# A three-block transformer kernel: weights ahead of tokens on the load queue, per-group waits for the first slots, and the first row maxima closed one phase earlier

## The reference

```python
x = x + 0.5 * L0_ffn(_layernorm(x))     # mixture of experts
x = x + L0_attn(_layernorm(x))          # causal softmax attention, 16 heads of width 16
x = x + 0.5 * L0_ffn(_layernorm(x))     # the same mixture of experts, same weights
x = x + 0.5 * L1_ffn(_layernorm(x))     # gated feed-forward with fp4-quantised activations and weights
x = x + L1_attn(_layernorm(x))          # causal linear attention
x = x + 0.5 * L1_ffn(_layernorm(x))
```

## Time and profile before

| | us |
|---|---|
| median of 3 executions | 2094.27 |
| lowest and highest | 2093.43, 2095.04 |
| the profiled execution | 2094.46 |
| its span in the trace | 2092.8 |
| PE busy, share of the span | 1996.7, 95% |
| DVE busy | 1478.9, 71% |
| ACT busy | 987.8, 47% |
| POOL busy | 927.5, 44% |
| end of the first-layer phase on PE (from the span's start) | 422.7 |
| first instruction of PE in the attention phase | 434.7 |
| end of the attention phase on PE | 910.3 |
| last slot's up_proj in the second layer begins | 1250.9 |

### The profile page before, as it was taken

How to read it: one execution, slowest core, us unless ns; L and a number is a source line. 1 busy time by engine, 2 the same in 40 slices (tenths; PEclk the granted TensorE clock), 3 DMA queues, 4 the chain that set the end, 5 groups by cost and what they waited for, 6 DMA issues and landing times.

```text
span 2092.8 us, 41681 instructions
## 1 busy us (share of the span) xinstructions
PE 1996.7 (95%) x13717; PEld 1400.7 (67%) x13717; DVE 1478.9 (71%) x4068; ACT 987.8 (47%) x2304; POOL 927.5 (44%) x1139
## 2 busy tenths in 40 slices
PE   6999999979999999987999998999999999899998
PEld 5999996534444444356899995776766666567776
DVE  6432555778888888643467648998877777698884
ACT  2333334346666666742334433333347777543432
POOL 5423655331111121213432566555557676556553
PEclk9999999989999999997999999999999999999999
DMA  6556655634443455013465662000000000000000
GB/s 199 199 196 211 241 203 136 167 62 54 62 59 46 51 62 62 2 45 136 135 209 194 222 203 68 1 0 0 1 1 2 2 2 2 2 11 20 10 21 21
DMA packets 101711, 173.59 MB, mean 83 GB/s; under 512 B 14704, under 2 KB 66320, under 8 KB 101520
## 3 DMA queue, kind: packets, MB, share of 16 engines
q1 hardware_dynamic: 95376, 154.40, 28.1%
q0 software_dynamic: 6144, 16.79, 2.3%
HBM read 136.01 MB, written 34.87 MB: 82 GB/s over the span
## 4 chain that ended last, share of the span: by engine, by line
PE 38%; DVE 13%; issue 3%; POOL 1%; ACT 1%; DVEq 0%; DMA 0%; SPq 0%; ACTq 0%; POOLq 0%
PE s_Y L805 5%; PE s_HH L793 5%; PE s_Y L1924 5%; PE s_R L1894 4%; PE s_HH L1894 4%; PE s_HH L2248 2%; PE s_R L2235 2%; PE s_Y L2327 1%; PE s_Y L2319 1%; DVE ff_hscale L1607 1%; DVE s_HH L1787 1%; PE s_R L2283 1%; DVE fw_down L1610 1%; PE s_R L2269 1%; PE s_R L1916 1%
## 5 line engine op out<-in xcount | busy, mean ns | idle before, releaser
L1023 DVE TENSOR_REDUCE part_max<-a_psS 128x1 f32<-128x512 f32 (+3 forms) x570 | 340.2, 655 | 74.2 <-PE a_psS L1016 66.1
L1558 ACT ACTIVATE a_PT<-a_psE 128x512 f32<-128x512 f32 (+1 forms) x608 | 308.9, 583 | 153.7 <-PE a_psE L1448 136.6
L1418 POOL TENSOR_SCALAR_AFFINE_SELECT a_PT<-a_PT 128x512 f32<-128x512 f32 x128 | 81.2, 634 | 376.4 <-ACT a_PT L1558 376.4
L1837 POOL TENSOR_TENSOR fw_down<-fw_down,ff_hm 128x704 f32<-128x704 f32 x64 | 97.4, 1522 | 226.2 <-DVE fw_down L1619 222.3
L1859 ACT ACTIVATE ff_hm<-fw_down 128x704 bf16<-128x704 f32 x64 | 50.6, 790 | 286.2 <-DVE fw_down L1610 286.2
L1924 PE MATMUL s_Y<-w_down,fw_up 128*128 128x256 f32 x768 | 178.0, 382 | 3.9 <-DVE X L1804 3.0
L1894 PE MATMUL s_R<-w_gate,ff_xqT 128*128 128x512 f32 (+1 forms) x512 | 165.7, 467 | 10.0 <-ACT ff_sil L1869 10.0
L1894 PE MATMUL s_HH<-w_up,ff_xqT 128*128 128x512 f32 (+1 forms) x512 | 162.5, 460 | 2.1 <-DVE fw_down L1610 2.1
L1924 PEld LDWEIGHTS s_Y<-w_down,fw_up 128*128 128x128 f32 x768 | 145.1, 191 | 21.4 <-issue 3.2
L1448 PE MATMUL a_psE<-sq,sk 98*128 98x512 bf16 (+3 forms) x528 | 153.3, 328 | 2.3 <-ACT a_PT L1558 1.4
L1464 PE MATMUL a_psO<-a_PT,a_va 128*32 128x512 f32 (+3 forms) x1536 | 150.4, 494 | 2.5 <-POOL a_PT L1418 1.8
(11 more groups left out here) (498 smaller groups left out, 4369.1 us busy)
## 6 DMA issues: line engine op xcount, KB each, us to landing
e_w<-w_in SPq DMA_DIRECT2D x35, 1024.0 KB, 5.0
sq<-w_in SPq DMA_DIRECT2D x18, 1024.0 KB, 5.1
sk<-w_in SPq DMA_DIRECT2D x17, 1024.0 KB, 5.1
e_xs<-sorted_x SPq DMA_DIRECT2D x70, 128.0 KB, 3.9
e_xr<-sorted_x SPq DMA_DIRECT2D x70, 128.0 KB, 4.3
sorted_y<-e_yo SPq DMA_DIRECT2D x70, 128.0 KB
sq<-qk_parts SPq DMA_DIRECT2D x66, 128.0 KB, 5.9
sk<-qk_parts SPq DMA_DIRECT2D x66, 128.0 KB, 6.4
```

The costliest lines, as they stand in the source:

```text
L1023: return dve.tensor_reduce(st.part_max[:, c, h0:h0 + heads, qt], scores[:, 0:heads * n].rearrange("p (h k) -> p h k", h=heads), AX.X, ALU.max)
L1418: pool.affine_select(out=hidden, in_=hidden, compare_op=ALU.is_ge, fill=0.0, base=0, pattern=[[0, HG], [1, P]], channel_multiplier=-1).the ...
L1558: act.activation(PT[kt % 2][:, h0:h0 + heads, q0:q0 + n], psE[e % RING][:, 0:heads * n].rearrange("p (h q) -> p h q", h=heads), ACT.Exp, s ...
L1837: c.link(pool.tensor_tensor(hv[i], hv[i], hm[i][:], ALU.subtract))
```

## The change

There are five edits.

1. The wait of the first slots is split. `scattered_first`, one semaphore for the first 12 (or 16) tiles, becomes one per group of four tiles. `load` of slot t waits for group (t + 3) // 4, each group once.
2. In `experts` the stage `load_weights` now stands ahead of `load` at the same depth, for all slots of both layers, and it takes over the wait for `ordered`.
3. SP stores hi as soon as `high` is there and mid as soon as `rest` is there. Only low still waits for `cut`; before, all three did.
4. Block 0's maxima are closed, turned, copied and stored in the first-layer phase, and the 9 lead pieces of block 1 are done there too. The score stages become 48 with start 4.6 and pace 0.1, instead of 38 with 4.8 and 0.11. The attention phase starts with its exponentials.
5. The semaphores are cleared, with the barrier behind that, only after the attention phase and at the end; the clearing and its barrier behind the setup and behind the first-layer phase are gone. The blocks' own barriers stay.

The core of the diff:

```diff
@@ -438,7 +440,7 @@
             if t % G == 0:
                 pool.wait_ge(placed, PLACED * (t // G + 1))
             pool.indirect_dma_start(st.sorted_x[:, :], bass.IndirectOffsetOnAxis(ap=st.slot[:, t:t + 1], axis=0),
-                                    XN[:, t, :], None).then_inc(scattered_first if t < FIRST_TILES else scattered, 16)
+                                    XN[:, t, :], None).then_inc(scattered_group[t // G] if t < FIRST_TILES else scattered, 16)
 
         return [(J, root, G), (J + 11, scatter)]
...
-    parts.scattered_first, parts.scattered = (scattered_first, 16 * FIRST_TILES), (scattered, 16 * (TILES - FIRST_TILES))
+    parts.scattered_group = [(s, 16 * G) for s in scattered_group]
+    parts.scattered = (scattered, 16 * (TILES - FIRST_TILES))
+    parts.filled_by = lambda slot: (slot + EXPERTS - 1) // G
...
@@ -747,13 +751,16 @@
             reuse(sp, turned, t)
             if t == 0:
                 sp.wait_ge(st.zeros_stored, 16)
+            if t == FIRST_SLOTS:
+                sp.wait_ge(*r.scattered)
+            elif t == 0 or t < FIRST_SLOTS and r.filled_by(t) > r.filled_by(t - 1):
+                sp.wait_ge(*r.scattered_group[r.filled_by(t)])
+            sp.dma_start(xs[p][:], st.sorted_x[bass.ds(row(sp, t), P), :]).then_inc(x_in[p], 16)
+
+        def load_weights(t, p):
+            reuse(sp, up, t, UP)
             if t in (0, FIRST_SLOTS):
                 sp.wait_ge(r.ordered, 2 * order_of(t) + 2)
-                sp.wait_ge(*(r.scattered if order_of(t) else r.scattered_first))
-            sp.dma_start(xs[p][:], st.sorted_x[bass.ds(row(sp, t), P), :]).then_inc(x_in[p], 16)
-
-        def load_weights(t, p):
-            reuse(sp, up, t, UP)
             e = sp.value_load(st.expert_of[0:1, order_of(t), bass.ds(t, 1)], min_val=0, max_val=EXPERTS - 1)
             sp.dma_start(w1[p], st.w1_in[bass.ds(e * D, D), :].rearrange("(k p) i -> p k i", p=P)).then_inc(w_in[p], 16)
...
-        return [(-1, load), (-1, load_weights), (1, load_residual), (4.25, store)]
+        return [(-1, load_weights), (-1, load), (1, load_residual), (4.25, store)]
...
-            dve.wait_ge(*r.scattered_first)
+            for group in r.scattered_group:
+                dve.wait_ge(*group)
             dve.wait_ge(*r.scattered)
...
+MAX = 4
+LEAD = 9
+
+
+def negative_maxima(dve, st, chain):
+
+    c, half = chain, BT // 2
+    c.link(dve.tensor_tensor(st.part_max[:, 0, :, half:], st.part_max[:, 0, :, half:],
+                             st.part_max[:, 1, :, half:], ALU.max))
+    c.link(dve.tensor_scalar(st.neg_max[:], st.part_max[:, 0, :, :], -1.0, None, ALU.mult))
+    flat = st.neg_max[:].rearrange("p h t -> p (h t)")
+    c.link(dve.tensor_copy(st.max_bf[:, 0, :], flat))
+    c.done(dve.tensor_tensor(st.max_bf[:, 1, :], flat, st.max_bf[:, 0, :], ALU.subtract))
+    c.end()
+
+
+def turn_maxima(pe, st, out):
+    return pe.transpose(out[:, 0:P // 2].bitcast(BF16), st.max_bf[:].rearrange("p a u -> p (a u)"), st.ident_bf[:])
+
+
+def copy_maxima(dve, st, it, turned):
+    return dve.tensor_copy(st.maxT[it % 2][:], turned[0:2 * HG * BT, 0:P // 2].bitcast(BF16))
+
+
+def store_maxima(sp, st, sq, it):
+
+    n = HG * BT
+    for a in (0, 1):
+        dst = sq[it % 3][SROWS + a:SROWS + a + 1, :, :].rearrange("o h (t q) -> o (h t) q", q=P)
+        sp.dma_start(dst, st.maxT[it % 2][a * n:(a + 1) * n, :]).then_inc(st.max_in[it % 3], 16)
+
...
@@ -1125,10 +1168,10 @@
 
     def sync(sp):
         def store(g, p, c):
-            sp.wait_ge(cut, g * CH + c + 1)
+            n = g * CH + c
             side, half = c // KD, c % KD
-
-            for part, src in enumerate((hi, mid, low)):
+            for part, (src, ready, value) in enumerate(((hi, high, n + 1), (mid, rest, 2 * (n + 1)), (low, cut, n + 1))):
+                sp.wait_ge(ready, value)
...
-            score_queries(pe, st, psS[u % SBANKS], st.sq[0], st.sk[0], pieces[u]).then_inc(scored, 1)
+            if u < S:
+                mm = score_queries(pe, st, psS[u % SBANKS], st.sq[0], st.sk[0], pieces[u])
+            elif u == S:
+                pe.wait_ge(padded, 1)
+                pe.wait_ge(maxed, MAX)
+                mm = turn_maxima(pe, st, psS[u % SBANKS])
+            else:
+                if u == S + 1:
+                    pe.wait_ge(st.stacked[1], 192)
+                mm = score_queries(pe, st, psS[u % SBANKS], st.sq[1], st.sk[1], pieces[u - S - 1])
+            mm.then_inc(scored, 1)
 
         return [(0, score)]
 
     def scores_vector(dve):
         def reduce(u, p):
+            if u == 0:
+                dve.memset(st.max_bf[:, 2:4, :], 0.0).then_inc(padded, 1)
             dve.wait_ge(scored, u + 1)
-            row_maxima(dve, st, psS[u % SBANKS], pieces[u]).then_inc(reduced, 1)
+            if u == S:
+                copy_maxima(dve, st, 0, psS[u % SBANKS]).then_inc(reduced, 1)
+                return
+            row_maxima(dve, st, psS[u % SBANKS], pieces[u if u < S else u - S - 1]).then_inc(reduced, 1)
+            if u == S - 1:
+                dve.wait_ge(reduced, S)
+                negative_maxima(dve, st, Chain(dve, maxed, MAX).at(0))
 
         return [(0.5, reduce)]
+
+    def scores_sync(sp):
...
+            if u == S:
+                sp.wait_ge(reduced, S + 1)
+                store_maxima(sp, st, st.sq, 0)
+
+        return [(0.75, store)]
 
     def end(sp):
         for s in stored:
             sp.wait_ge(s, 48 * NG)
 
     parts = Part(NG, 2, sync=sync, tensor=tensor, scalar=scalar, vector=vector, gpsimd=gpsimd)
-    return parts, Part(len(pieces), 1, tensor=scores_tensor, vector=scores_vector), normalize_vector, normalize_gpsimd, end
+    return parts, Part(SCORE_STEPS, 1, tensor=scores_tensor, vector=scores_vector, sync=scores_sync), normalize_vector, normalize_gpsimd, end
 
 
...
     RING = 8
-    SCORES_AT, SCORES_PACE = 4.8, 0.11
...
             r.sync(sp)
-            interleave(sp, of(e, "sync", 0, sp), of(q, "sync", Q, sp))
+            interleave(sp, of(e, "sync", 0, sp), of(q, "sync", Q, sp), between("sync", sp))
             end(sp)
 
...
 
-        if it < 0:
-            yield "max", 0, 0
-            for u in range(LEAD):
-                yield "s", 1, u
-            return
         for j in range(E if it < ITS else 8):
...
-        for it in range(-1, ITS + 1):
+        for it in range(ITS + 1):
...
             def maxima(it):
                 sp.wait_ge(s_drained, s_place["max", it, 0] + 1)
-                n = HG * BT
-                for a in (0, 1):
-                    dst = sq[it % 3][SROWS + a:SROWS + a + 1, :, :].rearrange("o h (t q) -> o (h t) q", q=P)
-                    sp.dma_start(dst, maxT[it % 2][a * n:(a + 1) * n, :]).then_inc(max_in[it % 3], 16)
-
-            maxima(0)
+                store_maxima(sp, st, sq, it)
+
             for it in range(ITS - 1):
...
     st.lin_bo_in = ins["lin_bo_in"]
 
+    own = []
+
+    def sem(name):
+        own.append(nc.alloc_semaphore(name))
+        return own[-1]
+
     def run(phase, *args):
-
-        own = []
-
-        def sem(name):
-            own.append(nc.alloc_semaphore(name))
-            return own[-1]
-
         phase(nc, st, sem, *args)
+
+    def free_semaphores():
         nc.clear_and_free_semaphores(own)
         nc.all_engine_barrier()
+        own.clear()
 
     st.sorted_x = nc.dram_tensor("sorted_x", [EXPERTS * REGION, D], F32, kind="Internal").ap()
     st.sorted_y = nc.dram_tensor("sorted_y", [SLOTS * P, D], F32, kind="Internal").ap()
```

More of the change, by code:

```diff
@@ L271, in route @@
     names = ("yturned yevac projected joined moment rooted normed turned evacuated logit choice ranked placed masked "
[L272 removed]
+             "scattered halved b1_turned "
              "placing1 table1 placing2 table2 ordered tabled").split()
     (yturned, yevac, projected, joined, moment, rooted, normed, turned, evacuated, logit, choice, ranked, placed, masked,
[L275 removed]
+     scattered, halved, b1_turned,
      placing1, table1, placing2, table2, ordered, tabled) = (sem(tag + n) for n in names)
+    scattered_group = [sem(tag + f"scattered_group{g}") for g in range(plan.first_tiles // 4)]
     MOMENTS, CHOICE, HIT, PLACED = 3, 7, 2, 4
@@ L1042, in queries_keys_values @@
     pieces = score_pieces()
+    S = len(pieces)
+    SCORE_STEPS = S + 1 + LEAD
     stored = [sem(tag + f"stored{c}") for c in range(CH)]
@@ L1470, in turn_max @@
                 out = free_s(s_place["max", it, 0])
-                pe.wait_ge(maxed, MAX * (it + 1))
-                pe.transpose(out[:, 0:P // 2].bitcast(BF16), max_bf[:].rearrange("p a u -> p (a u)"),
-                             st.ident_bf[:]).then_inc(s_filled, 1)
+                pe.wait_ge(maxed, MAX * it)
+                turn_maxima(pe, st, out).then_inc(s_filled, 1)
             def turn_out(it, c):
@@ L2504, in build @@
         st.stacked = [nc.alloc_semaphore(f"stacked{i}") for i in range(3)]
+        st.max_in = [nc.alloc_semaphore(f"max_in{i}") for i in range(3)]
```

51 lines of the change are left out of this document (19 added, 32 removed).

## The result

| | before | after |
|---|---|---|
| median | 2094.65 | 2294.03 |
| lowest and highest | 2093.43, 2095.66 | 2289.17, 2303.48 |
| the profiled execution | 2094.46 | 2289.17 |
| its span | 2092.8 | 2287.5 |

The change makes the kernel slower by 9.6%: the ratio is 1.096, 95% interval 1.0944 to 1.0976. That is +199.4 us of the medians and +194.7 us of the two spans. The forecast was +170.4. The four executions of the changed kernel lie further apart than those before, and the longer ones show a lower mean granted clock (2289.17 us at 0.975, 2303.48 at 0.969); the trace is that of the shortest.

A forecast was written before the change was run, and what follows sets the result against it. PE, busy 95% of the span, was taken to bound the kernel. Token waits of 174.2 us in 63 slots, less 2.0 and 1.8 for the starts, plus 0 for edits 3 to 5, gave +170.4: 2265 us, range 2225 to 2390.

The forecast's parts named there:

- the forecast's own range: 2228 to 2295 us for the whole kernel, from landings of 3.7 to 4.7 us and edits 3 to 5; chance 0.68.
- edits 3 to 5: Stores, maxima and clearing together: 4.6 - 3.0 - 1.6 = 0 us, with bounds of -7 and +5.
- Steady slots: Slots 8 to 34 of the first layer, 12 to 34 of the second: PE waits 50 x 2.95 = 147.5 us for tokens.
- 2.53 us of cover: Experts' steady step: the time from the weights' issue to when PE needs the tokens.
- Early slots: Slots 2 to 7 of the first layer lack 13.3 us; slots 2 and 6 to 11 of the second 13.4.
- Starts: First tokens of each layer go out sooner but behind 1 MB of weights: gains of 2.0 and 1.8 us.
- the price of a slot: Steady experts' step: tokens issued 1.18 us behind the weights land after 4.3, against 2.53 available; PE waits 2.95 us.
- rival (a): PE's clock falls in the new gaps; if in all 63, 2.5 us each and 2422 us; chance 0.20.
- the 6.01 us gap: PE idle gap in the trace before; matmuls behind it ran at granted clock 0.51, costing 2.5 us beyond its length.

The follow-up runs named there:

- tokens_first: The changed kernel with edit 2 taken back, so tokens stand ahead of weights again in every slot; 2088.94 us, ratio 0.9975.
- swap_alone: The kernel before with edit 2 alone, the wait for `ordered` moved to `load_weights`; 2311.54 us, ratio 1.1046.
- filler: The changed kernel with ten idle transposes on PE ahead of the wait for the tokens, from slots 6 and 10 on; 2286.10 us, ratio 1.0935.
- filler20: As filler, with twenty idle transposes in place of ten; 2288.74 us, ratio 1.0928.
- late_scores: tokens_first with the score pieces placed as before the change (start 4.8, pace 0.11); 2083.02 us, ratio 0.9942.
- halves: The changed kernel with a slot's weights as two DMAs of 512 KB and the tokens between them; 2261.91 us, ratio 1.0795.
- reads_first: The changed kernel with SP reading expert and row first, then issuing weights and tokens back to back; 2437.94 us, ratio 1.1678.
- half_only: As halves, but from slot 2 on the second half of the weights is not loaded (a probe, no usable kernel); 2209.63 us, ratio 1.0549.

## Why the prediction was right, and where its size was off

- **Right: what the edit does, and why.** The loss is the tokens' place behind the weights. tokens_first and swap_alone show it from both sides.
- **The number.** 2294 lies inside the forecast's own range of 2228 to 2295, but by luck: that range was made of landings of 3.7 to 4.7 us and of edits 3 to 5. With the waits as they were measured (+162.1) and no other term the sum would have given 2257. What filled the rest was not in it.
- **Steady slots.** Forecast 50 x 2.95 = 147.5 us; measured 135.8, 2.72 each. The landing was 4.1 and not 4.3 us. The 1.18 us between the issues and the 2.53 us of cover held. The period of 10.4 us came out as 10.0 in the first layer (203.91 to 213.94), whose step before is 7.25 us and not the 7.47 of the second; the sum counts waits alone and is not touched by that.
- **Early slots.** Forecast 13.3 and 13.4; measured 13.5 and 14.4.
- **Starts.** Forecast -2.0 and -1.8. By PE's waits 0.8 and 0.8 of it came (4.09 to 3.28, 4.79 to 4.01); slot 0 is turned at 46.93, where "about 46" was said. In the second layer it is turned 0.8 us sooner behind the table, but the table is ready 1.5 us later behind the attention's last transposes, so "2 us sooner" did not come: it is 0.67 later. The landing behind the first weights took 4.9 us from the issue (42.05 to 46.93) and not 4.2.
- **Edits 3 to 5.** Forecast 0. By the table of stretches -0.4 + 1.9 + 1.6 + 0.7 = +3.8, inside the bounds of -7 and +5. The details held: PE waits 1.74 us for the maxima (2.2 said) and 2.89 for the first stack (2.6 said), and the first `weigh` stands 10.7 us behind POOL's first memset where it was 13.6: 2.9 us sooner (3.0 said), with POOL late next. What was not in the sum is +1.6 in the attention stage, where the first `weigh` x16 takes 2.56 us and not 1.92. The same 1.6 us appear in filler, filler20 and late_scores, and not in tokens_first or halves.
- **The step that was off** is the price of a slot, "PE then waits 1.18 + 4.3 - 2.53 = 2.95 us", taken as all that a slot loses. PE's work around the wait was put at nothing; it grew by 31.7 us. Some 13 us of it are 0.22 us at every gap, at full clock, which no rival had either. Some 18 us are the clock, which I had treated as all or nothing: no fall in the sum, all 63 in rival (a). It fell in 14 steps. The waits in all grew by 162.1 us where 170.4 were forecast, so 31.7 - 8.3 = 23.4 of the 24.3 us that the forecast lacks against the profiled span are this term less that surplus. The cost of one fall was taken from the 6.01 us gap, 2.5 us. In the change it is 1.0 to 1.6 us in L800, and up to 2.7 in reads_first.
- **The two-term sum holds in every run without filler.** Growth of the waits plus growth of PE's busy time against the difference of the spans: 193.8 and 194.7 (after), 218.7 and 216.8 (swap_alone), 339.4 and 338.1 (reads_first), 167.4 and 168.3 (halves), 114.8 and 114.0 (half_only). In each of them some 13 to 14 us of the growth of PE's work are not the clock's, by an estimate of 0.22 us a gap from the steps at 1.00.
- **Open:** what decides whether the clock falls in a given gap. halves has shorter gaps than the change and more falls (17 against 12), swap_alone nearly the same gaps and 22. The last stretch of the second layer is 3.4 us shorter than before in the change and 2.1 in tokens_first; the cause is open.

## What to carry to other kernels

On a queue that works in strict order, put the small transfer that is needed next ahead of the large one that is needed a step later, above all when the large one has to wait for a buffer; splitting the large one helps less than the bytes suggest. When an edit opens a gap on PE in every step, price it as the gap, plus the overlap lost at its edges, plus slower work behind it; PE's busy time at equal instruction counts gives the last two together, and the steps whose clock stayed at 1.00 tell them apart. A gain found together with a loss has to be taken apart: here one edit of five cost 205 us and another gained 8.

## What I had not expected of the hardware

- 0.66 us more of idle time per step (2.63 to 3.29) took PE from 12 slow L800 of 58 to 47 of 58 and its granted clock in one stretch from 1.00 to 0.75; 1.26 us of useless transposes in each gap then took 79.7 us off the kernel.
- A gap costs 0.22 us more than its length even at a granted clock of 1.00 (7.47 us of PE work a step in place of 7.25).
- A transfer of 128 KB that was issued 1.1 us behind 512 KB landed after 3.1 us; with another 512 KB issued 0.5 us behind it, after 3.7.
